# Gating routed rows before they are stored, adding them in the gather, and another order in the attention, in a kernel of attention and experts

## What is computed

```python
xn = layernorm(x)
# attention: 16 heads of 8, decay per head, a state carried along the sequence
r, k, v = project(mix(xn, shifted xn))          # three 128x128 products with bias
A = (r @ k.T) * Wmat                            # within a chunk
y = A @ v + (r @ state) * wb                    # within, and from the chunks before
state = ws * state + (k * wk).T @ v
s = y @ Wo.T + bo
# experts: 8 shared ones for all tokens, 8 routed ones, two of them for a token
probs = softmax(xn @ gate_W.T); top_v, top_i = top_k(probs, 2)
routed = sum over the two of top_v * expert(xn) # expert: (silu(xn w1) * (xn w3)) w2
ffn = 0.5 * shared / 8 + 0.5 * routed
out = x + s * silu(ffn)
```

## Time and profile before

| | us |
|---|---|
| median of 3 runs | 815.15 (815.0 to 815.2) |
| the profiled execution | 814.67 |
| its span in the trace | 812.9 |

### The profile page before, as it was taken

One profiled execution on the slowest core, in us unless ns is written; L12 is line 12 of the kernel. 1 busy time (PEld: TensorE's weight loads), 2 busy tenths in 40 slices (PEclk: granted clock), 3 DMA queues, 4 the chain that ended last, 5 costly groups with the idle time before them and its releaser, 6 DMA issues. The chain is left out here.

```text
span 812.9 us, 25178 instructions
## 1 busy us (share of the span) xinstructions
PE 690.6 (85%) x9536; PEld 566.5 (70%) x9536; DVE 619.5 (76%) x1263; ACT 444.1 (55%) x946; POOL 441.4 (54%) x535
## 2 busy tenths in 40 slices
PE   3678998999999999999999999868777776777764
PEld 2466887999888899999999999745444444445443
DVE  6999997887568877777777777446888768887687
ACT  6765766655666666666666666623433334333331
POOL 2434997760444544444444444066667776677763
PEclk9999999999999999999999999989999999999997
DMA  9833320000223222222222224121222232222322
GB/s 246 239 96 110 116 69 20 29 27 28 60 66 77 82 66 67 63 68 63 67 60 68 67 64 63 46 63 31 73 67 73 69 112 76 67 73 70 110 64 60
DMA packets 79061, 61.73 MB, mean 76 GB/s; under 512 B 10498, under 2 KB 70276, under 8 KB 78948
## 3 DMA queue, kind: packets, MB, share of 16 engines
q1 hardware_dynamic: 70308, 42.41, 17.5%
q0 software_dynamic: 8640, 17.71, 9.2%
HBM read 38.20 MB, written 21.89 MB: 74 GB/s over the span
## 5 line engine op out<-in xcount | busy, mean ns | idle before, releaser
L483 POOL DMA_INDIRECT srows<-normed_rows,source x142 | 137.8, 971 | 188.4 <-PE banks L1235 141.2
L604 ACT CAST hidden<-hidden 128x512 f16<-128x512 f32 x206 | 127.3, 618 | 159.3 <-DVE hidden L955 157.9
L961 DVE TENSOR_TENSOR hidden<-hidden 128x512 f16<-128x512 f32 x194 | 133.8, 690 | 77.3 <-ACT hidden L604 57.3
L955 DVE TENSOR_TENSOR hidden<-hidden,banks 128x512 f32<-128x512 f32 x206 | 140.6, 683 | 26.6 <-ACT hidden L599 17.9
L1277 PE MATMUL banks<-sxh,wwords 128*128 128x256 f16 x568 | 154.9, 273 | 2.1 <-issue 1.9
L1278 PE MATMUL banks<-sxl,wwords 128*128 128x256 f16 x568 | 154.8, 273 | 0.0
L1279 PE MATMUL banks<-sxh,wwords 128*128 128x256 f16 x568 | 154.8, 273 | 0.0
L1294 PE MATMUL banks<-wwords,hidden 128*128 (+1 forms) x824 | 145.2, 220 | 7.2 <-DVE hidden L961 3.5
L1295 PE MATMUL banks<-wwords,hidden 128*128 (+1 forms) x824 | 144.8, 220 | 0.0
L1296 PE MATMUL banks<-wwords,hidden 128*128 (+1 forms) x824 | 144.7, 220 | 0.0
L599 ACT ACTIVATE hidden<-banks 128x512 f32<-128x512 f32 x206 | 122.2, 593 | 6.3 <-PE banks L1279 6.0
(11 more groups left out here) (183 smaller groups left out, 1511.9 us busy)
## 6 DMA issues: line engine op xcount, KB each, us to landing
sorted_results<-ybuf SPq DMA_DIRECT2D x71, 128.0 KB
rows<-x SPq DMA_DIRECT2D x32, 256.0 KB, 5.4
normed_rows<-rows SPq DMA_DIRECT2D x16, 256.0 KB, 3.7
r_rows<-rows SPq DMA_DIRECT2D x32, 128.0 KB
stage<-r_rows SPq DMA_DIRECT2D x16, 256.0 KB
out<-rows SPq DMA_DIRECT2D x16, 256.0 KB
srows<-normed_rows,source POOLq DMA_INDIRECT x142
stage<-w1e SPq DMA_DIRECT2D x8, 256.0 KB, 2.8
```

The costliest lines, as they stand in the source:

```text
L483: G.indirect_dma_start(srows[:, r % NXB, t, :], None, rows_in, bass.IndirectOffsetOnAxis(source[:, r * TPU + t:r * TPU + t + 1], 0)).then_ ...
L604: A.copy(guh[:, v % 2, h * 2 * UNIT:(h + 1) * 2 * UNIT], gu[:, i % 2, :]).then_inc(sem["gu_hi"], 1)
L955: V.tensor_tensor(gu[:, i % 2, :], sg[:, i % 2, :], psum[2 * (i % 2) + 1][:, :], ALU.mult).then_inc(sem["gated"], 1)
L961: V.tensor_tensor(gul[:, v % 2, s], gu[:, i % 2, :], guh[:, v % 2, s], ALU.subtract).then_inc(sem["gu_lo"], 1)
```

## The change

The change has five parts.

1. The rows of `normed_rows` get eight more floats, 136 in place of 128. SP writes the eight gate weights of every token there (`sp_probs`, in shared unit 16, pieces of 32 bytes), and the gather for the routed units brings them along with the row.
2. `dve_slot_gate` picks with two small operations for each routed unit the weight of the unit's expert, and `act_down` multiplies by it, in two products of 128x128 in place of one of 128x256. So the rows in `sorted_results` are gated already. A unit's DVE operation on `srows` must be done before POOL gathers into that place again.
3. `pool_fetch` adds while it gathers: the first and the second expert's rows are added by the DMA straight onto the tile `ffn`, the second ones after all four first ones of that step have landed. `pool_add`, `act_gated`, `dve_moe` and the tiles `picked` and `mo` are gone.
4. `pe_kv` takes k with tokens on partitions from `k32` by two transposes for each half, and computes only v by its 14 products, now of 128 columns. It waits for `k32`.
5. The order of POOL, ACT, DVE and PE in the attention loop is written anew.

```diff
+    RW = P + EXPERTS
+    rows_in = nc.dram_tensor("normed_rows", (NTOK, RW), F32, kind="Internal").ap()
...
+            def sp_probs():
+                nc.sync.wait_ge(sem["gates"], 1)
+                nc.sync.dma_start(rows_in[:, P:RW].rearrange("(t p) e -> p t e", p=P), probs[:, :, :]).then_inc(sem["probs_out"], 16)
...
+                if v == PROBS_AT:
+                    sp_probs()
...
+                    G.wait_ge(sem["probs_out"], 16)
                     G.wait_ge(sem["source"], 1)
                 if r >= NXB:
                     G.wait_ge(sem["s_flipped"], r - NXB + 1)
+                    G.wait_ge(sem["gate_picked"], r - NXB + 1)
...
+            def pool_fetch(u, b, k):
                 t = tile(u, b)
+                if k == 0:
+                    if (u, b) == (0, 3):
+                        G.wait_ge(sem["y_out"], NU)
...
+                    done = sem[f"first{u % 4}"]
+                else:
+                    G.wait_ge(sem[f"first{u % 4}"], 64 * (u // 4 + 1))
+                    done = sem[f"moe{u % 4}"]
+                G.indirect_dma_start(ffn[:, t, :], None, rows_out, bass.IndirectOffsetOnAxis(pos[:, t, k:k + 1], 0),
+                                     compute_op=ALU.add).then_inc(done, 16)
...
+                    A.wait_ge(sem["slot_gate"], r + 1)
...
-                    A.mul(ybuf[:, r % NYB, :, :].rearrange("p t d -> p (t d)"), src, 1.0 / SW / SW).then_inc(sem["y_out"], 1)
+                    for t in range(TPU):
+                        i = A.mul(ybuf[:, r % NYB, t, :], src[:, t * P:(t + 1) * P], slot_gate[:, r % GRING, t:t + 1])
+                    i.then_inc(sem["y_out"], 1)
...
+            def dve_slot_gate(v, step):
+                r = v - SHARED
+                if step == 0:
...
+                    V.tensor_tensor(picked_gate[:, r % 2, :, :], srows[:, r % NXB, :, P:RW], rep_mid(eun[:, r, :], TPU),
+                                    ALU.mult).then_inc(sem["gate_picked"], 1)
+                else:
+                    V.wait_ge(sem["gate_picked"], r + 1)
...
+                    V.tensor_reduce(slot_gate[:, r % GRING, :], picked_gate[:, r % 2, :, :], AX, ALU.add).then_inc(sem["slot_gate"], 1)
...
+                T.wait_ge(sem["k32"], u + 1)
                 for s in range(2):
                     b = 2 * i + s
-                    o = psum[0][:, s * 256:(s + 1) * 256]
-                    T.matmul(o, f2[:, :], brw[:, 0:256], start=True, stop=False)
+                    T.transpose(psum[0][:, 2 * s * P:(2 * s + 1) * P], k32[:, u % 2, b * P:(b + 1) * P], C("ident"))
+                    o = psum[0][:, (2 * s + 1) * P:(2 * s + 2) * P]
+                    T.matmul(o, f2[:, :], brw[:, P:2 * P], start=True, stop=False)
...
-                            j = T.matmul(o, a, m[:, 3 * shift + 1:3 * shift + 3, :].rearrange("p a d -> p (a d)"),
-                                         start=False, stop=(n == 5))
+                            j = T.matmul(o, a, m[:, 3 * shift + 2, :], start=False, stop=(n == 5))
...
             for u in range(-2, NA + 3):
-                if at(u - 2):
-                    dve_end(u - 2)
-                if at(u + 1):
-                    dve_kdec(u + 1, 0)
...
+                if at(u + 1):
+                    dve_decay(2 * (u + 1), 0)
+                    dve_state(2 * (u + 1))
...
```

More of the change, by code:

```diff
@@ L173, in build @@
         zsum = sb("zsum", [P, NT])
-        gates = [sb(f"gates{k}", [P, NT]) for k in range(2)]
         incl = take([P, EXPERTS, NT])
@@ L330, in build @@
         POOL_LOWS = 12
+        PROBS_AT = 16
         def low_done(engine, i):
@@ L508, in pool_low @@
                 G.tensor_tensor(in_order(yl, u, p), by_chunk(y32, u, p), in_order(yh, u, p), ALU.subtract).then_inc(sem["y_lo"], 1)
[L510 to L516, removed]
-                t = tile(u, b)
[L518 to L526, removed]
-                G.tensor_tensor(p0, p0, of_unit(u, ffn), ALU.add).then_inc(sem["first_added"], 1)
+            def pool_fetch(u, b, k):
+                t = tile(u, b)
+                if k == 0:
+                    if (u, b) == (0, 3):
+                        G.wait_ge(sem["y_out"], NU)
+                        for i in range(NYB):
+                            G.wait_ge(sem[f"y_stored{i}"], 16 * len(range(i, ROUTED, NYB)))
+                    done = sem[f"first{u % 4}"]
[4 more added lines that the diff above has]
+                                     compute_op=ALU.add).then_inc(done, 16)
             pool_prologue()
@@ L674, in act_high @@
                 A.copy(in_order(yh, u, p), by_chunk(y32, u, p)).then_inc(sem["y_hi"], 1)
-            def act_gated(u):
-                A.wait_ge(sem[f"picked{u % 2}"], 16 * 8 * (u // 2 + 1))
-                if u == 0:
-                    A.wait_ge(sem["gates"], 2)
-                for b in range(4):
-                    t = tile(u, b)
-                    A.mul(picked[0][:, u % 2, b, :], picked[0][:, u % 2, b, :], gates[0][:, t:t + 1]).then_inc(sem["first_gated"], 1)
             def act_moe(u):
                 s = u % 2
-                A.wait_ge(sem["moe"], 4 * (u + 1))
+                A.wait_ge(sem[f"moe{u % 4}"], 64 * (u // 4 + 1))
                 if u >= 2:
-                    A.wait_ge(sem["res"], u - 1)
-                A.activation(gt[:, s, :], mo[:, s, :, :].rearrange("p b d -> p (b d)"), ACT.Silu).then_inc(sem["moe_silu"], 1)
+                    A.wait_ge(sem["s_read"], u - 1)
+                A.activation(gt[:, s, :].rearrange("p (b d) -> p b d", b=4), of_unit(u, ffn), ACT.Silu).then_inc(sem["moe_silu"], 1)
             act_rates()
@@ L718, in act_program @@
             for u in range(-2, NA + 3):
+                if at(u - 1):
+                    act_mask(u - 1, 0)
+                    act_mask(u - 1, 1)
+                    act_v(u - 1, 0)
+                if at(u - 2):
+                    act_high(2 * (u - 2))
+                if at(u - 1):
+                    act_v(u - 1, 1)
                 if at(u):
-                    act_mask(u, 0)
-                    act_mask(u, 1)
+                    act_mask(u, 2)
+                    act_mask(u, 3)
                 if at(u - 2):
@@ L1062, in dve_inter @@
                                 rep_mid(wb[:, :], 4 * CH), ALU.mult).then_inc(sem["yint"], 1)
-            def dve_moe(u):
-                s = u % 2
-                V.wait_ge(sem["first_added"], u + 1)
-                if u >= 2:
-                    V.wait_ge(sem["moe_silu"], u - 1)
-                for b in range(4):
-                    t = tile(u, b)
-                    V.scalar_tensor_tensor(mo[:, s, b, :], picked[1][:, s, b, :], gates[1][:, t:t + 1], picked[0][:, s, b, :],
-                                           ALU.mult, ALU.add).then_inc(sem["moe"], 1)
             def dve_gate(u):
@@ L1141, in dve_program @@
                         dve_split(v, h)
+                    if h == 0 and SHARED <= v + 1 < NU:
+                        dve_slot_gate(v + 1, 1)
                     if i < 5:
@@ L1174, in dve_program @@
                     dve_select(2 * (u + 1))
+                if at(u + 2):
+                    dve_kdec(u + 2, 0)
+                if at(u - 1):
+                    dve_end(u - 1)
+                if at(u + 2):
+                    dve_decay(2 * (u + 2), 1)
+                if at(u):
+                    dve_gate(u)
+                if at(u + 2):
+                    dve_kdec(u + 2, 1)
         @block.tensor
```

103 lines of the change are left out of this document (52 added, 51 removed).

## The result

The changed kernel takes 840.19 us (median of 4 runs, 838.48 to 843.12) where the kernel before takes 815.17 beside it: a ratio of 1.031, 95% interval 1.028 to 1.034. The forecast of 791.5 lay on the wrong side, and the time lies outside its range. The profiled execution has a span of 838.1 us, 25.2 more than before.

What follows compares the result with a forecast made beforehand. It took a loop of waits between DVE and PE to bound the attention, 16.92 us a step. Twelve steps at −1.69, −1.7 for the first two, +0.8 start and −2.5 tail gave −23.7: 791.5 us, own range 781 to 802, overall 757 to 816.

Steps and rivals of the forecast that it cites:

- Routed stage, 0: Routed experts: split ACT product and two small DVE operations a unit cost 0 while PE stays ahead; all on path +30.
- A gather at 1.25: POOL in the attention: an adding gather costs the same as a plain one, 0.95 and 0.30 of issue.
- the second rival: Attention, POOL: adding gathers dearer, step 8f + 2.84, slower than before from f = 1.76; at f = 2.20, 857 us; chance 0.11.
- the 15.24: Forecast length in us of one attention step after the change, down from 16.92 by −1.69.
- −1.25: DVE in each attention step: the four multiply-adds of L1071 go, saving 1.25 us of DVE's 9.84.
- −0.54: PE in each attention step: first half of kv shortened by narrower products, less two added transposes, saving 0.54 us.
- a fact of this place: Attention: DVE's decay starts 3.60 us after the even local products' row ends on PE; unexplained and assumed to stay.
- Rival one: Attention: the 3.60 us late release goes and POOL's 12.84 is the step; 763 us (757 to 772); chance 0.20.
- Rival three: Attention: lateness moves to the odd local products, 1.7 us a step come back; 812.5 us (805 to 822); chance 0.11.
- Rival four: Routed stage: the fine store of probabilities holds up the r stores by its whole bound; 805.5 us; chance 0.06.
- Start and tail: Attention's ends: start +0.8 us as kv waits for k32 (0.3 to 1.7); tail −2.5 (0 to −5.2).
- The forecast's signs of being right: Attention: steps about 15.2, DVE waiting about 3.5 us a step for even local products, no L1071, kv's first half about 1.0.

Runs made afterwards that it cites:

- the run with the short kv: Kernel before with 10 of the 14 products of the second half of kv left out: 764.94 us beside 765.79 (0.997).

## Why the prediction was wrong, step by step

- *Routed stage, 0.* The largest error, 19.9 us. I read PE's 296.27 of 299 as "only PE's own work counts" and weighed ACT's and DVE's additions by their totals, which have room. The additions were no larger than bounded: on ACT 0.62 for the two products in place of 0.377, on DVE 0.17 and 0.16. But the stage is a hand-over between three engines in step, and PE's queue has a read that is hidden only while DVE's signal comes early, so a unit that took 4.18 takes about 4.44 in the middle of the stage. The bound, +30 with all of it on the path, was named, and then not used for the range.
- *A gather at 1.25.* It is 1.84, past the 1.76 from which the second rival said that the kernel is slower. That rival had the place; its price of 2.20 was too high, and its chance too low. Its reason, pieces that POOL writes one by one, is not borne out, and "the same 128 rows" was the wrong argument against it: with half the rows the queue's packets fell from 22976 to 14784 and the gather by 0.15. The thirteen middle steps of the attention take 17.55 on the mean, POOL's 17.6, in place of 16.93; the first step is 1.2 and the last 3.0 shorter. That is the 3.9. On the chip of 766.01, where nothing else is late, the price shows whole: 814.67 without gating, with adding gathers, against 763.36 with the gating and plain ones. On a chip of 819 plain gathers made it slower still (860.67), so the price alone did not keep the 15.24 away.
- *−1.25 and −0.54 a step.* Each was sized rightly (no L1071; kv of 1.1) and each is worth nothing by itself on a chip of 815, as the runs that take them one by one show. The step that failed is "I take it as a fact of this place": I summed a chain through a wait whose cause I didn't know. The wait was what gave way: with the shorter kv the decay starts 4.1 after the products' row in place of 3.60, and without L1071 the wait moves to the gate and kdec.
- *Rival one* came about only on another chip and with another gather. Plain gathers gave POOL's step and 763 there; 860 elsewhere. That it is the very number is chance, since that run's routed stage is 17 us longer than the 0 that the sum had for it.
- *Rival three*, the lateness on the odd local products, did not come: DVE's decays wait 3.4 us in 4 times for local products (560 to 800), though POOL may hide what would come without it.
- *Rival four* was wrong: the fine store landed in 8.0 us, not the 26.5 of the bound, and the r stores kept their pace of about 5 across it (144.62 to 149.81, by SP's timeline). The issues of the kernel after (count, KB each, median us to landing):

```profile
normed_rows<-rows SPq DMA_DIRECT2D x16, 256.0 KB, 4.7
...
normed_rows<-srows SPq DMA_DIRECT2D x1, 256.0 KB, 8.0
```

  The Trainium skill (DMA: Bandwidth & Descriptors, Specifications) asks for 512 bytes or more for line rate. The trace agrees in direction, as the same 256 KB in pieces of 512 bytes land in 4.7. The loss was too small to hold up the r stores, and the bound on it was mine, worked out from the earlier trace rows.
- *Start and tail* were small, as said, though not of the sign: −1.0 for the start and +0.6 for the tail.

The forecast's signs of being right did not come: POOL's gathers are 1.84 apart and not 1.25, DVE's waits of 3.4 for the even local products are gone, and the mean step of 17.2 is above the 16 at which I had called myself wrong in the main.

What stays open is the cause of the late signals. On most chips PE's signals come 3.6 us (with plain gathers up to 6.3) after the records end, whatever SP or the products queued behind do; half as many products bring the signal nearer, which speaks for their own work, but that the records are too short is not shown. In the six profiles from the two chips of 766 no such wait occurs. There, in the run with the short kv, the row of even local products ends at 580.04 and the decay that waits for it starts 0.11 later:

```profile
578.92 1.12 PE L1406 MATMUL banks<-wwords 32*64 32x256 f32 x32
```

```profile
580.15 1.23 DVE L1039 TENSOR_TENSOR wwords<-banks,wmat 128x1024 f32<-128x1024 f32 x1 [0.17 <-PE banks L1406]
```

The Trainium skill (TensorE: Matmul & The Clock Gate, Part 3, "The cost: per-tile semaphore tail") has 126 ns for 16 products with one increment, and the trace of that run is near it with 32.

## What to carry to other kernels

An engine at 99% of a stage doesn't make the other engines' work free there: look at how early each hand-over comes, and price an addition on an engine that hands over as if it were on the path until a row shows the slack. Don't count a gain on a chain that runs through an unexplained wait; first take the gain alone, as a run, and see whether the wait gives it back. And price a new kind of DMA by a run or by both ends: a gather that adds held POOL half as long again as a plain one.

## What the runs showed of the hardware

An adding gather of 128 rows of 512 bytes holds POOL for 1.54 to 1.58 us, a plain one for 0.95 to 1.00; with 64 rows the adding one still takes 1.43. The queue that POOL feeds moved 22976 packets in the kernel after and 8640 in the one before, for as many gathers. In the attention the mean granted clock fell from 1.00 to 0.88 where PE waited up to 4.8 us a step for POOL: in one step it was 0.50 (1.2 GHz) from 683 to 689, where PE waited for POOL's mask from 681.0 to 685.56; from 676 to 682, with PE busy 4.82 of 6 us, it was 1.00 (2.4 GHz). And one program took 766 us on two chips and 811 to 821 on others. By the nearest profile of the first kind, the run with the short kv, all but 1 us of the difference lies behind the routed stage, in the attention with its many small f32 products.
